# A transformer block on one core: second `M` block after block behind the first row tiles, low parts of the shared weights by rows, slot work in other places

## The reference

```python
h = _layernorm(x) * (1 + ca) + sa
Q, K, V = split(_layernorm(h) * gamma + beta) @ W_in + b_in
K = _rotary(K); V = _rotary(V)
A = 0.5 * sum(_cos_sim(K) * _cos_sim(V), rows) + 0.5
x = x + ga * ((A[:, None, :] * Q) @ W_out + b_out + h)
h = _layernorm(x) * (1 + cb) + sb
...
topk_w, topk_idx = top_k(softmax(h @ gate_w), 2)
routed = sum over the two experts of topk_w * ((silu(h @ w_gate[e]) * (h @ w_up[e])) @ w_down[e])
shared = silu(h @ sw_gate) * (h @ sw_up) @ sw_down
x = x + gb * (routed + shared)
```

## Time and profile before

| | us |
|---|---|
| median of the runs | 694.96 (693.85 to 696.95, 3 runs) |
| the profiled execution | 692.15 |
| its span | 690.4 |
| TensorE busy | 650.5 (94%) |
| VectorE busy | 495.0 (72%) |
| ScalarE busy | 269.3 (39%) |
| GpSimd busy | 166.4 (24%) |

### The profile page before, as it was taken

The page is one execution under the profiler, slowest core; times in us unless marked ns, Lnnn a source line. Parts: engine busy times, 40 slices in busy tenths (PEclk is TensorE's granted clock), DMA queues, the critical chain, the costliest instruction groups (busy, mean ns, idle before and its releaser), DMA issues.

```text
span 690.4 us, 10579 instructions
## 1 busy us (share of the span) xinstructions
PE 650.5 (94%) x3666; PEld 534.1 (77%) x3666; DVE 495.0 (72%) x1099; ACT 269.3 (39%) x525; POOL 166.4 (24%) x211
## 2 busy tenths in 40 slices
PE   7699999999997799999699999999999999999995
PEld 3477677777765687788588788889889899898894
DVE  4887789835798878556876765459678696786953
ACT  3554354535432332322101301426447364564531
POOL 1223233310021111100000002203555435563133
PEclk9999999999998999999899999999999999999998
DMA  8912121104253522413023035336667666686144
GB/s 332 394 29 100 49 76 35 42 4 165 74 171 107 205 102 83 152 47 107 1 77 130 1 96 156 92 132 204 106 168 197 103 199 108 170 182 116 45 62 61
DMA packets 41151, 80.80 MB, mean 117 GB/s; under 512 B 5019, under 2 KB 13229, under 8 KB 40566
## 3 DMA queue, kind: packets, MB, share of 16 engines
q1 hardware_dynamic: 33382, 62.06, 27.0%
q0 software_dynamic: 7728, 18.22, 14.3%
HBM read 58.88 MB, written 22.56 MB: 118 GB/s over the span
## 4 chain that ended last, share of the span: by engine, by line
PE 60%; DVE 20%; issue 8%; ACT 5%; DMA 3%; SPq 1%; POOL 1%; POOLq 0%; ACTq 0%; DVEq 0%
PE bank L1755 17%; PE bank L1757 16%; PE bank L1756 16%; PE bank L2052 3%; DVE gtR L1664 1%; DVE gsel L1632 1%; PE bank L1885 1%; DVE st L1104 1%; DVE rows L1318 1%; PE bank L1821 1%; PE bank L1803 1%; DVE ht L1620 1%; DVE hx L1330 1%; ACT ht L963 1%; DMA sgraw<-in_L_ffn_sw_up 1%
## 5 line engine op out<-in xcount | busy, mean ns | idle before, releaser
L1755 PE MATMUL bank<-xt,sgu 128*128 128x512 f32 x176 | 71.4, 406 | 10.1 <-DVE sgu L1088 9.7
L1755 PE MATMUL bank<-ht,ew 128*128 128x256 f32 (+1 forms) x256 | 74.2, 290 | 0.0
L667 POOL DMA_INDIRECT out_rows<-y,si x35 | 54.8, 1565 | 77.3 <-DVE y L1684 69.5
L1756 PE MATMUL bank<-ht,ew 128*128 128x256 f32 (+1 forms) x256 | 73.1, 285 | 0.0
L1757 PE MATMUL bank<-ht,ew 128*128 128x256 f32 (+1 forms) x256 | 73.0, 285 | 0.0
L1757 PE MATMUL bank<-xt,sgu 128*128 128x512 f32 x176 | 70.3, 400 | 0.0
L1756 PE MATMUL bank<-xt,sgu 128*128 128x512 f32 x176 | 70.3, 399 | 0.0
L1755 PE MATMUL bank<-wkv,xt 128*128 128x512 f32 x128 | 53.9, 421 | 2.2 <-DVE xt L1133 2.2
L1756 PE MATMUL bank<-wkv,xt 128*128 128x512 f32 x128 | 50.5, 394 | 0.0
L1757 PE MATMUL bank<-wkv,xt 128*128 128x512 f32 x128 | 50.4, 394 | 0.0
L647 POOL COPY gi<-gidx 128x5 int32 (+1 forms) x8 | 7.7, 963 | 174.0 <-DVEq L1593 134.2
(11 more groups left out here) (373 smaller groups left out, 1639.2 us busy)
## 6 DMA issues: line engine op xcount, KB each, us to landing
xring<-in_L_attn_X SPq DMA_DIRECT2D x32, 256.0 KB, 2.8
ewst<-in_L_ffn_w_gate SPq DMA_DIRECT2D x8, 704.0 KB, 5.1
ewst<-in_L_ffn_w_up SPq DMA_DIRECT2D x8, 704.0 KB, 4.9
slots<-in_L_wmod SPq DMA_DIRECT2D x4, 1024.0 KB, 7.2
x_d<-rows SPq DMA_DIRECT2D x16, 256.0 KB, 2.0
h_d<-hx SPq DMA_DIRECT2D x16, 256.0 KB, 2.0
xrow<-x_d SPq DMA_DIRECT2D x16, 256.0 KB, 2.8
out_rows<-xrow SPq DMA_DIRECT2D x16, 256.0 KB, 2.0
```

The costliest lines, as they stand in the source:

```text
L667: pool.indirect_dma_start(out=out, out_offset=bass.IndirectOffsetOnAxis(ap=si[0:CR[j], par, j:j + 1], axis=0), in_=y[0:CR[j], j, :], in_of ...
L1755: nc.tensor.matmul(dst, a[0], b[0], start=first, stop=False)
L1756: nc.tensor.matmul(dst, a[0], b[1], start=False, stop=False)
```

## The change

Nothing is computed otherwise, but for four new small factors and two operations fewer in `y_bias`. What is moved:

- At the start tile 1 is normalised, turned and split (`normed`, `tokens_hi`, `tokens_lo`) ahead of the second bias row and of the table product. `x_statistics(2)` goes behind the product.
- The first matrix is multiplied block by block (`m_first`), and VectorE takes each block when it is done, between the readings of batch 1 (`a1`, `scaled_q_lo`). Before that stand the `bc_c` products and the statistics vectors `nm1` and `std1`. `y_factors` makes two factors for the bias, used in `y_bias` (six operations before, four now).
- The second matrix (`m_second(k)`, 12 matmuls for each k) stands, for k = 1 to 3, behind `y_matmul(0)` to `y_matmul(2)`. The first three tiles use buffers of their own (`rows0`, `hx0`, `u0`), since `swq` and `wo` are alive still. ScalarE reads the second matrix at tiles 4 and 5 instead of 0 and 1.
- `shared_in_lo` goes by k: four operations of 128x1408 at tiles 0 to 3.
- In the routing, `expert_order` and `slot_counts` stand at chunk 2, `slot_entries` and `row_ranks` at chunk 3, `row_entries` at chunk 4, `entry_experts` behind `slots()`. `gathered` works on both chosen experts at once, two operations of 256 elements instead of four of 128.
- In an expert unit, `select_gb` of places 2 and later and `turn_columns` stand behind `expert_rows` of the first places.

The diff, cut to what the steps name:

```diff
 Y_CHUNKS = {6: 0, 9: 1, 12: 2, 14: 3}
-SHARED_LO = {5: 0, 8: 1, 10: 2, 13: 3, 14: 4, 15: 5}
...
             bias_row_hi(0)
             weights_hi(1, (1, 2, 3))
+            normed(1)
             bias_row_hi(1)
-            normed(1)
+            tokens_hi(1)
             act.wait_ge(sincos, 1)
...
+            a_rows(1)
+            m_block_hi(0, 0)
             act.wait_ge(st_ready, 1)
             x_normed(0)
             x_normed(1)
+            m_block_hi(0, 1)
+            act.wait_ge(w_mm, NT)
+            scaled_q(1, 0)
+            m_block_hi(0, 2)
+            for k in range(1, DC):
+                scaled_q(1, k)
+            m_block_hi(0, 3)
...
-                if t < 2:
-                    m_block_out(2 * t)
-                    m_block_out(2 * t + 1)
+                if t in (FIRST + 1, FIRST + 2):
+                    m_block_out(2 * (t - FIRST - 1))
+                    m_block_out(2 * (t - FIRST - 1) + 1)
...
-            def shared_in_lo(m):
-
-                dve.wait_ge(sg_hi, DC)
-                parts = [slice(at + m * P, at + (m + 1) * P) for at in (0, UP_COL)]
-                if m == NS - 1:
-                    parts = [slice(m * P, UP_COL)]
-                for at in parts:
-                    last = dve.tensor_tensor(sgu[:, 1, :, at], sgraw[:, :, at], sgu[:, 0, :, at].bitcast(F32),
-                                             ALU.subtract)
-                last.then_inc(sg_lo, 1)
+            def shared_in_lo(k):
+
+                dve.wait_ge(sg_hi, k + 1)
+                dve.tensor_tensor(sgu[:, 1, k, :], sgraw[:, k, :], sgu[:, 0, k, :].bitcast(F32), ALU.subtract)\
+                    .then_inc(sg_lo, 1)
...
             bias_rows(1)
-            x_statistics(2)
+            tokens_lo(1)
             dve.wait_ge(table_in, 32)
             dve.tensor_tensor(cos, cos, sin, ALU.mult).then_inc(sincos, 1)
+            x_statistics(2)
...
+            def y_factors():
+
+                for b in range(B):
+                    at = slice(b * Q4, (b + 1) * Q4)
+                    dve.tensor_copy(comb_ga[at, :], bc_ga[at, b, :])
+                    link(dve.tensor_tensor(comb_s[at, :], bc_s[at, b, :], bc_ga[at, b, :], ALU.mult))
...
+                if t < DC:
+                    shared_in_lo(t)
                 if t in Y_CHUNKS:
                     s_mul_of(0, Y_CHUNKS[t])
-                if t in SHARED_LO:
-                    shared_in_lo(SHARED_LO[t])
...
-                        (slot_counts, slot_entries, slot_ranks)[m - 2]()
+                        if m == 2:
+                            slot_counts()
+                            expert_order()
+                        elif m == 3:
+                            slot_entries()
+                            row_ranks()
+                        else:
+                            row_entries()
...
                     slots()
+                    entry_experts()
...
-                    for place in GB_AT[-1]:
-                        select_gb(u, par, last, place)
-                    if ahead:
-                        turn_columns(u + 1, 1 - par)
                     for place in range(tiles_of(par, last)):
                         expert_rows(u, par, last, place)
+                        if place == 1 and ahead:
+                            turn_columns(u + 1, 1 - par)
+                        select_gb(u, par, last, place + 2)
...
+            def m_second(k):
+
+                pe.wait_ge(swq_lo, DC + k + 1)
+                for i in range(DC):
+                    if k == 0 and i >= 2:
+                        pe.wait_ge(m32_ready, i - 1)
+                    last = m_part(1, i, k)
+                last.then_inc(mk_mm, 1)
...
-            m_matmul(0, (0,))
+            m_first(0)
             weighted_sums(NT - 1)
-            m_matmul(0, (1,))
+            m_first(1)
             misc("a1")
-            m_matmul(0, (2, 3))
+            m_first(2)
+            m_first(3)
             pe.wait_ge(misc_read, len(MISC))
             h_matmul()
-            m_matmul(1)
+            m_second(0)
...
                     if m == 0:
                         pe.wait_ge(t2_lo, GT * (g + 1))
                         if g == 0:
+                            pe.wait_ge(sg_lo, DC)
                             pe.wait_ge(m_out, DC)
-                    if g == 0:
-                        pe.wait_ge(sg_lo, m + 1)
...
             for t in range(NT):
                 y_matmul(t)
+                if t < DC - 1:
+                    m_second(t + 1)
```

171 lines of the change are left out of this document (96 added, 75 removed).

## The result

| kernel | us, median (lowest to highest) | profiled execution, its span |
|---|---|---|
| before | 695.24 (693.85 to 696.95) | 692.15, 690.4 |
| changed | 672.23 (671.45 to 675.52) | 675.52, 673.7 |

The ratio is 0.967, its 95% interval 0.964 to 0.971: 3.3% faster. The prediction was 671.5 for the median and 668.5 for the profiled run. The profiled execution of the changed kernel is the longest of its runs, 3.3 us above their median and 7.0 above the 668.5; that of the kernel before is 3.1 under its median.

The account below looks back on a forecast made before the run. TensorE's work was taken as the floor, with gains where it waits for VectorE. The sum -1.0 - 11.3 - 6.9 - 4.1 - 0.3 = -23.6 gave a median of 671.5 us; 8-in-10 range 665 to 683.

Parts of the forecast that it names:

- Start: Start: tile 1 ahead of the tables brings tile 2's turn from 36.97 to 35.95; gain 1.0, between 0 and 2.4.
- up to 0.9 may come on top: Start: GpSimd's power of tile 1 no longer beside the table product, 1.46 against 0.55; start would then give 1.9.
- Crossing: Crossing to the second rows: less VectorE work behind the last `swq`, shorter `y_bias`; `bc_s` load and tile 0's rows 6.1 sooner.
- Low parts: Second rows: `shared_in_lo` at tiles 0 to 3 removes `sgu` waits and slow clock; -11.3 with the crossing's 6.1.
- Routing: Routing: product 5.7 sooner, slow clock's 1.9 gone, 0.7 paid at the shared rows; -6.9, between -5 and -8.
- Experts: Expert units: two of four `gsel` products behind `y` remove TensorE's seven waits; -4.1, between 0 and -4.5.
- A: Second rows: VectorE bounds, low parts at tiles 0 to 3 pay front back; -4 instead of -11.3, 678.7; chance 0.18.
- B: Expert units: the seven waits for `y` turn into others of the same length; 675.5; chance 0.14 for B or C.
- C: Routing: `entry_experts` holds the shared rows longer than 0.7, routing gives 3; 675.3; chance 0.14 for B or C.
- D: Start: tile 2 sets the start, which then gives nothing; 672.5; chance 0.08.
- E: Tile 3 to chunk 0: short TensorE waits bring 1.2 GHz, which stays through the shared part; 701; chance 0.03.
- signs of being wrong: Wait over 2 us at first shared rows behind routing; VectorE's tile 15 later than 268; clock 0.8 with short waits only.

Follow-up runs that it names:

- the second trace of the changed kernel: The changed kernel run once more without any edit: 672.39 us median, ratio 0.969 to before; its profiled execution took 675.47, span 673.7.
- the first trace: The changed kernel's first profiled execution, against the kernel before: 675.52 us, span 673.7.
- the last kernel above: The changed kernel with the start as before and `entry_experts` moved behind the first one-hots: 670.48 us, ratio 0.968 to before.
- the second comparison: The changed kernel, no edit, measured again against the kernel before: 672.39 us, ratio 0.969 (0.967 to 0.970).
- the third, with the statistics sooner: The changed kernel with the statistics of tile 2 moved ahead of the table product, behind the low part of tile 1: 672.44 us.

## Why the prediction was right

The places of the gains were right, and three of five terms came out near their size. That the sum of 23.6 meets 23.0 is in part luck: the start and the routing were too large, together by 2.6, and the traces show less than the medians do. The profiled run was forecast at 668.5 and took 675.52.

**Start, forecast 1.0, measured 0.2, or a loss of 1.4.** The step that failed is "its turn at 36.97 is what waits next; I let it come at 35.95". It came at 35.84, as said, and the matmuls of tile 1 began at 31.54 in the start alone, 2.3 sooner. But ScalarE has the reading of `cs` behind the normalising step that was late, and TensorE waits 0.40 for it; that was not asked. And in some executions TensorE falls to the 1.2 GHz level behind these two waits, which costs 1.6 us. The estimate "up to 0.9 may come on top" from GpSimd held as far as the operation (1.46 to 0.55), not as far as the time, and the 1.9 named beside it for the start did not come.

**Crossing, forecast 6.1, measured 6.2.** 18.29 to 12.11 with the two parts alone, 11.98 in the second trace of the changed kernel. The y bias begins 1.85 sooner instead of 3.3 in the first trace, in which the whole run is 1.2 late from the start; without that it is 3.1, and the load of `bc_s` is issued 5.8 sooner. What the forecast did not ask is that the load itself now holds the rows (3.32 of waiting in the first trace), so that only what brings its issue forward would still bring the rows forward.

**Low parts, forecast 5.2 of 11.3, measured 4.7 to 5.7, and some 2 in the one trace of the low parts alone.** The price of the operation (1.62 forecast, 1.62 measured) and the cadence (6.0, measured 5.98) were right, and so is the timetable of TensorE. Chunk 0 was put at 209.5, chunk 1 at 227.2, chunk 2 at 244.0, chunk 3 at 257.4. In the last kernel above, whose start is that of before, they stand at 209.57, 227.33, 244.46 and 258.01: 10.7 sooner than the 268.71 of before, where 11.3 was forecast. In the first trace of the changed kernel they are later by the start (1.2) and the load of `bc_s`: chunk 0 at 211.11, chunk 3 at 259.54. TensorE's short waits, 1.5 for `rows` and 2.0 for `xt` or 0.5 and 1.5 for `mw`, lie where VectorE sets the pace, and chunk 1 starts 17.76 behind chunk 0 with either, where 17.7 was forecast. The lower clock that "may still be met" is there, from 204 to 208, in the tiles ahead of chunk 0. It costs nothing: VectorE's stretch of the second rows is 88.9 in each trace with these parts, with and without it.

**Routing, forecast 6.9, measured 5.1.** The wait (0.55), the slow clock (gone) and the 0.7 at the shared rows (shown as 0.78, costing 0.95) were right; until there TensorE has gained 7.4 where the forecast has 7.6. The failed step is that the cost of `entry_experts` was asked for at one place only. It holds the one-hots as well, and two waits of 0.3 and 0.5 cost 1.34 of the missing 1.8. Moved behind the first one-hots it costs nothing there.

**Experts, forecast 4.1 and 0.3 for the end, measured 4.7 and 0.** To take the lost time and not the idle time was the right reading: the 2.9 us of waits alone would have been too small by more than a third. The lost time per wait was still put too low. Ahead of the restarted matmul 0.17 more is lost than is shown as idle, as forecast, and the step behind it is 0.34 instead of 0.23 (484.00 to 484.34); over the seven waits the gain is 0.26 each on top of the idle time. The 0.3 at the end did not come: the last `y` starts 0.49 behind the last matmul with the experts' part as without it.

**The rivals.** A (VectorE bounds the second rows) and B (another wait for `y`) are out. C was right in kind and smaller in size, 1.8 instead of 3.9, with the cost at the one-hots more than at the shared rows. D, given a chance of 0.08, was right: the start does nothing, and its 672.5 is nearer to the 672.23 than the 671.5 is. E, the clock, has shown itself where the forecast did not look, at the start, and is free where it looked: it fell at 204 us and did not stay low, with 1.00 from 220 us on.
The Trainium skill, "TensorE: Matmul & The Clock Gate", section "HAM oscillation — how this bites in real kernels", warns of gaps in TensorE's work that come back and return it to half rate. The traces agree that gaps in the work bring the lower level (0.62 of full speed behind the 4.8 of before). They show it also behind shorter ones (1.32 and 0.40 close together, and the waits of tiles 3 and 4), but not each time (three traces of five at the start).

**The signs.** Tile 1's turn came at 26.50, the cadence is 5.98, no wait for `sgu`, none over 2.5 and none of the seven for `y` is left, `gtS` has 0.6, the clock is 1.00 from 220 to 280. The rows of tile 0 came at 179.41 instead of 177. Of the signs of being wrong two stand in the first trace: VectorE's tile 15 is at 268.31, just behind 268 (267.1 without the 1.2 of the start), and the clock is 0.62 and 0.57 at 36 and 204 us, where only short waits are. The first means no more than the start's loss, the second is the price told above.

**What the medians say more.** The parts add up in the stretches to 0.2 + 10.9 + 5.1 + 4.7 = 20.9, and in the medians of the four kernels with one part each to 0.3 + 10.4 + 5.3 + 6.6 = 22.6. The changed kernel has 18.8 less in the stretches of its second trace and 19.8 with the start as before, but 23.0 less in the medians, 21.9 in the second comparison, and 20.6 in the third, with the statistics sooner. So the forecast of 23.6 is above each of these numbers. The profiled run of before (692.15) lies 3.1 under its median, that of the changed kernel 3.3 above. Each of the four ratios of the parts has an interval of 1.5 to 1.8 us to either side, so that the two sums do not contradict each other. The place of the slow stretches and the first transfers make a part of the spread: tile 1's turn lies between 27.7 and 29.9 us in the seven traces with the old start, 8.7 behind tile 0's where the clock is full and 10.0 to 10.2 where it falls at 20. What the runs without a trace spend beyond the traces of before is left open.

## What to carry to other kernels

A wait of the bounding engine costs more than its idle time: add the restart (0.26 us here for each of seven), and the slow matmuls behind a long one (1.9 us after 6.1). When work is moved, look for everyone who waits behind its new place, down to the second and third consumer: here `entry_experts` cost 0.95 us at the first and 1.34 at the next two, and a step of 2.6 us found a place where no wait for it is left. Look also at what the new order leaves last: the crossing now ends with a load. TensorE's clock fell in the first 40 us with the old and the new order, at different places; take more than one trace before a slow stretch is laid to the change.

## What was not expected of the hardware

- TensorE's clock fell to the 1.2 GHz level behind waits of 1.32 and 0.40 us in three of five traces with that order, and not in the other two with the same waits. The forecast held 1.4 us to be harmless. In the first 40 us it fell somewhere in ten of fourteen traces, and where decides what it costs: 1.3 to 1.6 us at 20, nothing at 28, 1.4 to 1.6 at 36.
- A slow stretch of TensorE that lies where VectorE sets the pace costs nothing at the end: 88.90 and 88.91 us for the second rows with it, 88.91 without.
- An operation of GpSimd of one element per partition took 1.46 us beside a VectorE product of 128x1024, which takes 1.22, and 0.55 without it. That was foreseen; new is that it did so in all nine traces with the two side by side and in none of the five without, in three orders of the work, and that the 0.9 us saved on GpSimd did not shorten the start.
- The time from the issue of a load to its first use changed between executions of the same kernel, and where the load ends the chain the time goes with it: in the two traces of the changed kernel 5.41 and 4.81 us for `bc_s` at the crossing, 9.23 and 7.75 for `sdraw`.
